# First block of a four-layer kernel: another order of the steps on four engines

## The reference, cut to what matters

```python
scores = jnp.einsum('bthd,bghd->bhtg', Q, K) / np.sqrt(DH)      # 4 heads, 77 keys
topv, topi = jax.lax.top_k(scores, 32)
attn = zeros.at[topi].set(softmax(topv));  attn_mean = attn.mean(axis=1)
c_t = einsum(attn_mean, V)
x = layernorm(x_text)
x = x * (1 + gate * scale_in) + gate * shift_in                  # scale, shift from c_t @ W_film
# s4d: a long convolution with a kernel that is made here
dtA = dt[:, None] * A;  dC = C * (jnp.exp(dtA) - 1.0) / A
K = 2.0 * einsum('dn,dnl->dl', dC, exp(dtA[:, :, None] * arange(L))).real
y = irfft(rfft(x) * rfft(K)) + x * D_skip
y = y * (1 + gate * scale_out) + gate * shift_out
```

## Time and profile before

| | us |
|---|---|
| median of 3 runs | 569.19 (566.96 to 569.96) |
| the profiled execution | 567.04 |
| its span, first to last instruction | 565.1 |
| TensorE busy | 488.2 (86%) |
| VectorE busy | 382.1 (68%) |
| ScalarE busy | 269.3 (48%) |
| GpSimd busy | 153.8 (27%) |

### The profile page before, as it was taken

One profiled execution on the slowest core, in us unless ns is written; L12 is line 12 of the kernel. 1 busy time (PEld: TensorE's weight loads), 2 busy tenths in 40 slices (PEclk: granted clock), 3 DMA queues, 4 the chain that ended last, 5 costly groups with the idle time before them and its releaser, 6 DMA issues. The chain is left out here.

```text
span 565.1 us, 9299 instructions
## 1 busy us (share of the span) xinstructions
PE 488.2 (86%) x3127; PEld 339.2 (60%) x3127; DVE 382.1 (68%) x1365; ACT 269.3 (48%) x819; POOL 153.8 (27%) x180
## 2 busy tenths in 40 slices
PE   2980699999979999988886768989999999989987
PEld 2330699897634666775553445766666666658845
DVE  3799979844683767745877446764544546689876
ACT  2599477512325666613453415642222221579653
POOL 4999983031134400012104531020000000020042
PEclk9995579999999999997899788999999999989999
DMA  7103000002190000000011030000000000000001
GB/s 268 51 1 149 1 3 1 2 0 73 78 391 37 2 1 2 1 2 1 0 35 45 1 100 1 2 0 2 2 0 1 0 1 1 1 1 1 2 0 38
DMA packets 8453, 18.37 MB, mean 32 GB/s; under 512 B 1171, under 2 KB 6611, under 8 KB 7894
## 3 DMA queue, kind: packets, MB, share of 16 engines
q1 hardware_dynamic: 8406, 17.78, 8.9%
HBM read 15.99 MB, written 1.79 MB: 31 GB/s over the span
## 5 line engine op out<-in xcount | busy, mean ns | idle before, releaser
L212 POOL TENSOR_SCALAR rtmp<-mv 128x4 f32<-128x4 f32 x22 | 5.1, 231 | 273.6 <-DVE mv L191 243.0
L1837 PEld LDWEIGHTS bank<-arenaA,arenaB 128*128 128x128 f32 x320 | 38.7, 192 | 8.5 <-issue 7.2
L1821 PE MATMUL bank<-xnT,arenaA 128*128 128x512 f32 x80 | 41.1, 595 | 0.7 <-ACT xnT L262 0.7
L1848 ACT ACTIVATE xt<-bank 128x512 f32<-128x512 f32 x26 | 15.5, 598 | 54.3 <-PE bank L1821 53.2
L1899 DVE TENSOR_TENSOR arenaB<-xt,bank 128x512 f32<-128x512 f32 x26 | 17.8, 686 | 34.5 <-PE bank L1822 31.8
L1822 PE MATMUL bank<-xnT,arenaA 128*128 128x512 f32 x80 | 40.8, 592 | 0.0
L1837 PE MATMUL bank<-arenaA,arenaB 128*128 128x128 f32 x320 | 38.8, 275 | 0.0
L255 PE MATMUL bank<-in_ctx 128*128 128x512 f32 (+1 forms) x100 | 35.4, 497 | 0.0
L1092 DVE TENSOR_REDUCE nmax<-bank 128x1 f32<-128x512 f32 x32 | 20.5, 684 | 13.2 <-PE bank L1035 13.2
L420 DVE MATCH_REPLACE8 arenaB<-arenaB 128x77 f32<-128x77 f32 x128 | 26.8, 223 | 0.0
L1822 PEld LDWEIGHTS bank<-xnT,arenaA 128*128 128x128 f32 x80 | 15.2, 190 | 19.1 <-issue 19.1
(11 more groups left out here) (484 smaller groups left out, 1289.8 us busy)
## 6 DMA issues: line engine op xcount, KB each, us to landing
arenaA<-in_moe_dram SPq DMA_DIRECT2D x1, 3840.0 KB, 11.6
in_dft<-in_dft_dram SPq DMA_DIRECT2D x1, 2048.0 KB, 7.4
in_dft<-in_head_dram SPq DMA_DIRECT2D x1, 2048.0 KB, 7.5
arenaA<-in_l_dram SPq DMA_DIRECT2D x1, 2048.0 KB, 16.1
vw_scratch<-in_dft SPq DMA_DIRECT2D x32, 38.5 KB
arenaB<-vw_scratch SPq DMA_DIRECT2D x2, 576.0 KB, 4.9
in_rows<-in_rows_dram SPq DMA_DIRECT2D x1, 842.5 KB, 7.5
in_ctx<-in_ctx_dram SPq DMA_DIRECT2D x1, 653.0 KB, 6.5
```

What stands on the lines that cost most here:

```text
L1821: nc.tensor.matmul(bank[n % 2][:], w[:, c * P:(c + 1) * P], xnT[:, b * S:(b + 1) * S], start=True, stop=True).then_inc(up_mm, 1)
L1837: ins = nc.tensor.matmul(bank[4 + m % 2][:, q4 * P:(q4 + 1) * P], hid2[:, m % 2, c, q4 * P:(q4 + 1) * P], w[:, 2 * HE + c * P:2 * HE + (c ...
L1848: nc.scalar.activation(sil2[n % 3], bank[n % 2][:], ACT.Silu).then_inc(silu_ready, 1)
```

## The change

It touches the order of work, not what is computed.

- GpSimd: the 24 instructions of the coefficients come ahead of the angles of columns and rows (new function `pool_s4_angles`). Then the first half of the normalised input, the gate, the four quarters of the rows, and the second half. The quarters wait for the last sine (E_GS), where they waited for the row exponentials.
- ScalarE: the row exponentials, group 0's exponentials and sums, and the fold's first copies come ahead of the sines. The diagonals of group 0 follow the sines, then the fold's second copies, group 1's exponentials and the weighing of group 0, all ahead of the first kernel quarter.
- VectorE: the top-32 of group 1 comes ahead of `vec_s4`, mask and weights of group 0 ahead of `vec_s4_columns`, and three more rounds of top-32 ahead of the film of group 1.
- TensorE: film 0, quarters 0 and 1, film 1, quarters 2 and 3; the fold in two parts, in banks 0 and 1.
- Buffers: the scratch of the columns' phase lies where the column sines are written later, so `vec_s4` drops one wait. The scaling has a semaphore of its own.

```diff
-        rH, hh4, eH = part(arenaB, 8416, D, LH), part(arenaA, 2176, D, LA), part(arenaA, 6272, D, LA)
+        rH, hh4, eH = part(arenaA, 2176, D, LH), part(arenaA, 2176, D, LA), part(arenaA, 6272, D, LA)
...
             dve.wait_ge(s4_pool, A_UG)
-            dve.wait_ge(s4_vec, V_H)
...
-            n = D // 4
+
+        def pool_s4_angles(pool):
+            tt, n = nc.gpsimd.tensor_tensor, D // 4
...
         def pool_s4_rows(pool, st, slices):
-            pool.wait_ge(s4_act, E_ROWS)
+            pool.wait_ge(s4_act, E_GS)
...
         def pe_fold1(pe):
             pe.wait_ge(*loaded["l1"])
-            pe.wait_ge(s0_copy, NT)
-            nc.tensor.matmul(bank[2][0:DC, 0:D], V["wk1"], V["wq1"], start=True, stop=True).then_inc(fold1_mm, 1)
-            nc.tensor.matmul(bank[3][0:DC, 0:D], V["wv1"], V["wo1T"], start=True, stop=True).then_inc(fold1_mm, 1)
+            pe.wait_ge(ln_T, NB)
+            nc.tensor.matmul(bank[0][0:DC, 0:D], V["wk1"], V["wq1"], start=True, stop=True).then_inc(fold1_mm, 1)
+            nc.tensor.matmul(bank[1][0:DC, 0:D], V["wv1"], V["wo1T"], start=True, stop=True).then_inc(fold1_mm, 1)
+
+        def pe_fold1_ctx(pe):
...
# TensorE
             pe_fold1(pe)
+            pe_fold1_ctx(pe)
+            pe_film(pe, 0)
             pe_kernel(pe, 0)
             pe_kernel(pe, 1)
+            pe_film(pe, 1)
             pe_kernel(pe, 2)
-            pe_film(pe, 0)
             pe_kernel(pe, 3)
-            pe_film(pe, 1)
+            pe.wait_ge(fold1_copy, 4)
             pe_dft_k(pe)
...
# ScalarE
-            act_x2(act)
-            act_s4_columns(act)
-            act_s4_turns(act)
             act_s4_rows(act)
             act_exps0(act, 0)
+            act_x2(act, 0)
             act_sums0(act, 0)
             act_vfilm(act)
             act_fold1(act)
+            act_s4_columns(act)
+            act_s4_turns(act)
+            act_diag(act, 0)
+            act_fold1_ctx(act)
+            act_exps0(act, 1)
+            act_weighed(act, 0)
+            act_sums0(act, 1)
+            act_film(act, 0)
             act_kernel(act, 0)
-            act_exps0(act, 1)
+            act_diag(act, 1)
+            act_x2(act, 1)
             act_kernel(act, 1)
-            act_sums0(act, 1)
-            act_diag(act, 0)
-            act_kernel(act, 2)
-            act_weighed(act, 0)
-            act_film(act, 0)
-            act_diag(act, 1)
-            act_kernel(act, 3)
             act_weighed(act, 1)
             act_film(act, 1)
+            act_kernel(act, 2)
+            act_kernel(act, 3)
...
# GpSimd
             pool_s4_gains(pool, st)
+            pool_s4_angles(pool)
+            pool_x2(pool, st, 0)
             pool_gate(pool)
             pool_s4_rows(pool, st, range(4))
-            pool_x2(pool, st, 0)
             pool_x2(pool, st, 1)
...
# VectorE
             vec_top(dve, st, 0, range(4))
+            vec_top(dve, st, 1, range(4))
             vec_s4(dve, st)
-            vec_s4_columns(dve)
-            vec_top(dve, st, 1, range(4))
             vec_mask0(dve, 0)
             vec_weight0(dve, st, 0)
+            vec_s4_columns(dve)
             vec_top(dve, st, 2, range(2))
             vec_mask0(dve, 1)
             vec_weight0(dve, st, 1)
             vec_film(dve, st, 0)
-            vec_top(dve, st, 2, range(2, 3))
+            vec_top(dve, st, 2, range(2, 4))
+            vec_top(dve, st, 3, range(1))
             vec_film(dve, st, 1)
-            vec_top(dve, st, 2, range(3, 4))
+            vec_top(dve, st, 3, range(1, 3))
             vec_mask0(dve, 2)
             vec_weight0(dve, st, 2)
-            vec_top(dve, st, 3, range(4))
+            vec_top(dve, st, 3, range(3, 4))
```

More of the change, by code:

```diff
@@ L529, in pe_dt @@
             nc.tensor.matmul(bank[7][:, 0:D], V["avg"], dtd, start=True, stop=True).then_inc(s4_pe, 1)
-        A_ARE, A_ANG, A_VH, A_UG, A_GAIN = 2, 3, 4, 5, 6
-        E_TANH, E_ANG, E_H, E_X2, E_COLS, E_GC, E_GS, E_ROWS = 1, 2, 3, 4, 6, 7, 8, 9
+        A_ARE, A_ANG, A_GAIN, A_VH, A_UG = 2, 3, 4, 5, 6
+        E_TANH, E_ANG, E_H, E_ROWS, E_COLS, E_GC, E_GS = 1, 2, 3, 4, 5, 6, 7
+        x2_act = sem("x2_act")
         def vec_dt_row(dve):
@@ L699, in act_kernel, with act_x2 @@
             ins.then_inc(kern_act, 1)
-        def act_x2(act):
+        def act_x2(act, b):
             act.wait_ge(twice_ready, 1)
[L706 to L709, removed]
+            for t in range(b * TB, (b + 1) * TB):
+                ins = nc.scalar.activation(tmp2[:, t, :], xn[:, t, :], ACT.Copy, scale=mv2[:, t:t + 1])
+            ins.then_inc(x2_act, 1)
         def pool_x2(pool, st, b):
             r = slice(b * TB, (b + 1) * TB)
-            pool.wait_ge(s4_act, E_X2 + b)
+            pool.wait_ge(x2_act, b + 1)
             pool.wait_ge(*loaded["rows"])
@@ L1174, in pe_fold1, with act_fold1_ctx @@
             pe.wait_ge(*loaded["l1"])
-            pe.wait_ge(s0_copy, NT)
-            nc.tensor.matmul(bank[2][0:DC, 0:D], V["wk1"], V["wq1"], start=True, stop=True).then_inc(fold1_mm, 1)
-            nc.tensor.matmul(bank[3][0:DC, 0:D], V["wv1"], V["wo1T"], start=True, stop=True).then_inc(fold1_mm, 1)
+            pe.wait_ge(ln_T, NB)
+            nc.tensor.matmul(bank[0][0:DC, 0:D], V["wk1"], V["wq1"], start=True, stop=True).then_inc(fold1_mm, 1)
+            nc.tensor.matmul(bank[1][0:DC, 0:D], V["wv1"], V["wo1T"], start=True, stop=True).then_inc(fold1_mm, 1)
+        def pe_fold1_ctx(pe):
             pe.wait_ge(fold1_copy, 2)
-            nc.tensor.matmul(bank[2][:, 0:NB * NC], a1[:], V["ctxT"][0:DC], start=True, stop=True).then_inc(fold1_mm, 1)
+            nc.tensor.matmul(bank[0][:, 0:NB * NC], a1[:], V["ctxT"][0:DC], start=True, stop=True).then_inc(fold1_mm, 1)
             for b in range(NB):
-                ins = nc.tensor.matmul(bank[3][0:NC, b * D:(b + 1) * D], V["ctxT"][0:DC, b * NC:(b + 1) * NC], bm1[:], start=True, stop=True)
+                ins = nc.tensor.matmul(bank[1][0:NC, b * D:(b + 1) * D], V["ctxT"][0:DC, b * NC:(b + 1) * NC], bm1[:], start=True, stop=True)
             ins.then_inc(fold1_mm, 1)
-            pe.wait_ge(fold1_copy, 4)
         def act_fold1(act):
             act.wait_ge(fold1_mm, 1)
-            nc.scalar.copy(a1[:], bank[2][0:DC, 0:D]).then_inc(fold1_copy, 1)
+            nc.scalar.copy(a1[:], bank[0][0:DC, 0:D]).then_inc(fold1_copy, 1)
             act.wait_ge(fold1_mm, 2)
-            nc.scalar.copy(bm1[:], bank[3][0:DC, 0:D]).then_inc(fold1_copy, 1)
+            nc.scalar.copy(bm1[:], bank[1][0:DC, 0:D]).then_inc(fold1_copy, 1)
+        def act_fold1_ctx(act):
             act.wait_ge(fold1_mm, 3)
-            nc.scalar.copy(m1[:], bank[2][:, 0:NB * NC]).then_inc(fold1_copy, 1)
+            nc.scalar.copy(m1[:], bank[0][:, 0:NB * NC]).then_inc(fold1_copy, 1)
             act.wait_ge(fold1_mm, 4)
-            nc.scalar.copy(vw1[:], bank[3][0:NC, 0:NB * D].rearrange("p (b d) -> p b d", b=NB)).then_inc(fold1_copy, 1)
+            nc.scalar.copy(vw1[:], bank[1][0:NC, 0:NB * D].rearrange("p (b d) -> p b d", b=NB)).then_inc(fold1_copy, 1)
         def pe_l1x(pe):
```

2 lines of the change are left out of this document (1 added, 1 removed).

## The result

The changed kernel takes 574.80 us (median of 20 runs, 569.25 to 578.64), the kernel before in the same session 568.83 us (20 runs, 566.53 to 569.96). The ratio is 1.009, with a 95% interval of 1.007 to 1.011: slower by about 6 us. The profiled execution took 573.74 us against 567.04, its span is 571.7 us against 565.1.

The account below looks back on a forecast made before the run. TensorE's dense block from L752 was taken as the bound. L752 moves from 85.8 to 93.0, so 567.0 + 7.2 = 574.2 us for the profiled execution and 576.4 for the median; range 570.5 to 582.5.

Parts of the forecast that it names:

- What bounds, and where the time shows: TensorE's dense block from L752: the change costs the shift of its start, +7.2 us, plus or minus the clock.
- GpSimd's gain and what becomes of it: GpSimd's coefficients: 11.7 us gained, given away to group 1's top-32 and the phases; quarters start at 58.5, before 55.9.
- The product beside the quarters: VectorE's L557 beside GpSimd's quarters: they exclude each other, seven pairs at 1.55 us, product done at 69.4.
- The rival without the alternation: VectorE's product not slowed beside GpSimd's quarters: L557 ends at 64.7, shift +2.3, 571.5 us; 15 in 100.
- The chain behind the weights: From group 1's weights at 79.7 through diagonals, weighing, film, two quarters and a copy to L752 at 93.0.
- low-clock rival: TensorE's clock rises only inside L752's stretch: L752 at 96.9, shift +11 to +13.5, 580.3 to 582.7 us; 20 in 100.
- one of my signs of being wrong: TensorE: a full clock between 69 and 81 would show the forecast wrong.
- The clock inside L753: Transform's first block on TensorE: clock rises within the film before it, same intervals as before from its start at 93.
- the other side: GpSimd's quarters the only bound: L752 at 82.3 to 83.9, shift -3.5 to -1.9, 565.7 to 567.3 us; 5 in 100.
- the 72 from which the gain would begin: VectorE's weights of group 1: ready before 72 decides for a faster kernel; the forecast has 79.7.

Follow-up runs that it names:

- gains_late: Changed kernel with GpSimd's coefficients behind the angles again; 575.88 us, ratio 1.0097 to the kernel before.
- gpsimd_alone: Kernel before with only GpSimd's coefficients moved ahead of the angles; 576.05 us, ratio 1.0122 to the kernel before.
- top1_back: Changed kernel with group 1's top-32 behind the column product again; 582.50 us in one run.
- rows_wait: Changed kernel with GpSimd's quarters also waiting for the end of VectorE's column product; 570.89 us, ratio 1.0032 to the kernel before.
- quarter2_first: Changed kernel, quarter 2 ahead of group 1's film, quarter 1's copy and second scaling ahead of group 1's diagonals; 570.88 us, ratio 1.0026 to the kernel before.
- wait_and_quarter2: Changed kernel with the edits of rows_wait and quarter2_first together; 573.36 us, ratio 1.0083 to the kernel before.
- spin_gap: Changed kernel with seven idle matmuls on TensorE ahead of the film of group 1; 574.24 us, ratio 1.0103 to the kernel before.
- weigh_after: Changed kernel with TensorE's and ScalarE's order of weighing and quarters as in the kernel before; 572.63 us, ratio 1.0077 to the kernel before.
- split_top: On rows_wait: group 1's top-32 split around phases and product, groups 0 and 1 ahead of group 2, group 1's diagonals ahead of copies; 571.12 us, ratio 1.0037.
- split_spin: split_top with four idle matmuls on TensorE ahead of film 0, quarter 1 and the transform; 567.93 us, ratio 0.9999 to the kernel before.

## Why the prediction was right, and where it wasn't

**What bounds, and where the time shows: right.** The shift of the kernel's transform carried to the end: +6.5 us at the second group of the transform (113.08 less 106.60), +6.6 in the span, +6.0 in the medians. I forecast +7.2, and 576.4 us for the median; it is 574.80.

**GpSimd's gain and what becomes of it: right.** The coefficients are done at 34.1 (forecast 34.6), the angles at 42.9 (43.2), the last sine ends at 58.3 (58.5). That the 12 us are worth nothing is shown by the 10.99 us in which GpSimd then waits, which gains_late repeats in the other order; that they are given to the top-32 of group 1, by gpsimd_alone and top1_back.

**The product beside the quarters: the mechanism right, the size a little high.** I took 1.55 us for a pair, 11.6 in all; the source view of the line says

```profile
L557 DVE TENSOR_TENSOR arenaA<-arenaA x8: 684/1541/1749, 57.4 to 66.3; 128x512 f32<-128x512 f32 x8
```

so the median was right and the sum 10.48, since one product ran before the first quarter at 0.68 us. The split of a small pair into 0.53 and 0.33 us came from no row: alone a product takes 0.61 us of the queue (rows_wait) and a coefficient step 0.45. The rival without the alternation is out by rows_wait: without GpSimd beside it the product takes 4.90 us. Measured from the first maximum, it ended 1.0 us earlier than I said (48.1 against 49.1), and the weights 1.6 us earlier (57.8 against 59.4). Of the other 0.6 us the trace shows only where small instructions happened to meet GpSimd: L417 of 128x8 took 1.20 us in this queue before and 0.17 here, while the two masks L427 took 1.94 and now take 2.70.

**The chain behind the weights: right.** 13.5 us from the weights to L753 (77.6 to 91.1), 13.3 forecast. The weighing ran at half clock as said, and the film took 3.10 us, between my 2.0 and 3.8. VectorE's film of group 1 came at 87.94 (I had 91), well covered. One step in front of the chain was wrong and cost nothing. I had quarters 0 and 1 at half clock, 2 x 3.57 us, over at 76.6. They ran full, from 68.17 on in 4.47 us, and were over at 72.6. So TensorE idled 6.33 us instead of four, and the full clock from 68 to about 75, one of my signs of being wrong, did appear in part. It was lost in that idle time (0.50 from 75 on), since TensorE waited for VectorE's weights.

**The clock inside L753: the term I mis-sized.** I let the clock stay full from the film on, and had more time in L753 only in the low-clock rival, "up to 2.5 us more there". It fell there without that rival: +1.7 us. The windows above show the sequence: full for six us in which TensorE was busy 4.85, mostly with quarters, and idle for the last 1.23 us, waiting for the copy; then a fall inside dense work. This took back the 1.4 us (by the ruler) by which L753 began earlier than forecast, so the sum came out better than its terms, and that part is luck. What makes the clock fall there is not shown. In quarter2_first, with one quarter ahead of the same idle time, L753 took 7.38, but in wait_and_quarter2, with one as well, 9.01; and in spin_gap it took 7.38 behind both quarters. In weigh_after, with the film just ahead and no idle time, it ran in 7.31.

**The low-clock rival and the other side: out.** L753 began at 91.1, not at 96.9, and the weights of group 1 came at 77.6, far from the 72 from which the gain would begin. rows_wait reached 72.1 and was still not faster. wait_and_quarter2 had the weights at 71.0 and only one quarter behind the film, and was held up by the order in front of it: the third quarter came from GpSimd at 75.7, and L754 began at 87.48. split_top had them at 70.5, with L754 at 84.80 and a fallen clock. So weights before 72 are not enough; the rest of the chain has to be short as well, and no kernel tried here had that.

**What stays open.** Why split_spin's median is 3.2 us under split_top's, with L754 at the same place and of the same length. What decides whether the clock falls at the kernel's transform. And how much of the changed kernel's wider scatter (9.4 us between its fastest and slowest run, 3.4 in the kernel before) is the clock's: two profiled executions can differ in a stage that no edit touches, as here the same 32 matmuls of a later stage (L1642 there, L1647 in rows_wait) in the kernel before and in rows_wait,

```profile
333.99 2.11 PE L1642 MATMUL bank<-kcT,arenaB 64*128 64x77 f32 x32
```

```profile
338.10 3.70 PE L1647 MATMUL bank<-kcT,arenaB 64*128 64x77 f32 x32
```

at a granted clock of 0.95 in the one and 0.50 in the other. But one execution of each is not a distribution.

## What to carry to other kernels

Before moving work on GpSimd or VectorE, write down what stands beside it on the other engine at the new place: VectorE's products of two inputs in SBUF took 4.90 us alone and 10.48 beside GpSimd, 24 coefficient steps took 11.9 us beside maxima and replacements, whose top-32 was hardly slower for it (12.4 us for group 0 beside the steps, 12.3 for group 1 beside the angles), and each meeting cost more beside GpSimd's 128x512 than beside its 128x128 instructions (10.48 against 6.87 us for eight). An engine made faster is worth what lies behind its next wait: find that wait first, here the last sine, 11 us away. And two edits that each win 3.9 us can win 1.4 together, when one was fitted to the lateness that the other removes.

## What the runs showed of the hardware that I had not expected

- The same eight products of 128x512 take 4.90 us with GpSimd idle (684 ns each), 6.87 beside 128x128 instructions and 10.48 beside 128x512 ones. GpSimd's own went from 1.06 to 1.50 us and from 1.27 to 1.59.
- Excluding each other is not only for instructions of two inputs: the phase's first step, one input and a scalar, took 2.27 us beside GpSimd's 128x512 products for the normalised input and 1.27 or 1.28 alone (split_top and the changed kernel, L541 with 128x2048).
- After 4.2 us of kernel quarters at full clock (TensorE busy 4.22 us with matmuls of 16 moving columns) and 1.2 us idle, the clock fell from the 2.4 GHz level to the 1.2 GHz one at the dense transform, whose 64 matmuls take 7.31 us at full clock. In the changed kernel it fell inside the transform (9.01 us); in rows_wait and split_top already in the idle time (granted 0.66 and 0.80 over it, 0.50 from the transform's first instruction on; 10.23 and 8.78 us). Behind the same quarters and idle time it did not fall in spin_gap (7.38 us).
